# Graph layers on one core: the adjacency loaded as bf16 through GpSimd's queue into six half-size buffers

## The chip, the cores and the metric

The kernel runs on one core of one Trainium2 chip. The metric is the device time of one execution, in microseconds (us). TensorE (PE, with its weight loads shown apart as PEld), VectorE (DVE), ScalarE (ACT) and GpSimd (POOL) compute; SyncE (SP) and GpSimd start DMA transfers, which 16 DMA engines carry out. The engines run on their own instruction streams and meet at semaphores.

## The reference

There are 4096 nodes with 128 features, and an int32 adjacency of 4096 x 4096 in which an entry is 1 with probability 1/256. Two layers follow one another:

```python
def _L0_gnn_ref(x, adj):            # for each row: the maximum over its neighbours
    mask = a != 0
    masked = jnp.where(mask[:, :, None], x[None, :, :], neg)
    m = jnp.max(masked, axis=1)
...
def _L1_gnn_ref(input, W, a, adj, M):
    h = input @ W
    e = jax.nn.leaky_relu((h[:M] @ a_src)[:, None] + (h @ a_dst)[None, :], negative_slope=ALPHA)
    valid = (adj[:M] > 0) & (h.sum(axis=1) != 0)[None, :]
    att = jax.nn.softmax(jnp.where(valid, e, NEG), axis=1)
...
    attention = jnp.where(att >= THR, att, 0.0) * L[:, None]
    h_prime = attention @ h
    return jax.nn.elu(h[:M] + h_prime)
x = _layernorm(x + _L0_gnn_ref(x, adj), axis=-1)
x = _layernorm(x + _L1_gnn_ref(x, L1_gnn_W, L1_gnn_a, adj, 4096), axis=-1)
```

## The kernel before

**Tiling.** The 4096 rows of the adjacency are 32 tiles of 128; four tiles (512 rows) are a group, so there are 8 groups. The 4096 columns are 33 segments of 126, put together in 6 parts of 6, 6, 6, 5, 5 and 5 segments (PARTS). A part of a group is one load: 128 partitions x 4 tiles x up to 756 int32 (1512, 1260 or 1136 KB), in rows of up to 3024 bytes.

**First phase, to about 690 us.** For each segment of each group TensorE transposes the four 126-column blocks into psT (turn, L864 to L878), ScalarE turns them into 0/1 in bf16 (evict, L684, tile at), TensorE ranks them (rank, L884), ScalarE makes a one-hot choice (heat, L692, tile hot), and TensorE selects rows of x with it by three bf16 matmuls (select, L900, psS), whose running maximum DVE keeps (best, L1227, acc). This gives the maximum over one neighbour of each segment for each row. Small matmuls (code, L911) collect where further neighbours are. One group later DVE ranks these codes (top_keys, decode, make_lists at steps s = 1 to 7), and GpSimd gathers the rows of x by index from DRAM: 20 direct gathers (gather_direct, L621) and 12 extra ones (gather_extra, L631), each 128 rows of 512 bytes. DVE takes them in with direct_max (s = 30 of the same group) and extra_rows (L1374, s = 4 of the next one); TensorE's route (L945) and acc_turn, and DVE's aggregate (y, L1390, s = 9) follow, then the layer norm, x1 and the heads for the second layer. GpSimd may begin the gathers of a group only when the previous group's acc_turn has been taken, which y's instruction tells it.

**Order.** All orders are written by hand: each engine walks through g (groups, two more than 8) and s (33 segments), and what belongs to group g-1 or g-2 stands at fixed s. TensorE is two turns ahead of the selection.

**Queues.** The adjacency lands in adj_in, three buffers of one part each (ADJ_RING = 3). SP's queue carries all plain transfers. SP issues load q+3 when part q has been turned (semaphore turned), then the store of part q of at to adjT_dram (L474), and at the fourth part of a group the store of x1 (L483) and the load of own (L479). GpSimd's queue carries the gathers only. One semaphore, at_stored, counts all stores of at; evict waits on it before it writes a part of at again.

**Second phase.** From about 690 to 1010 us the attention reads at back from adjT_dram and reuses adj_in's bytes as wbuf (three float32 buffers; the total size of adj_in stays the same under the change). Then one block of rows is worked out exactly, and the kernel ends.

The code of the parts named is printed here.

## Time and profile before

| what | value |
|---|---|
| median of 3 runs | 1084.57 us (1081.44 to 1092.72) |
| the profiled execution | 1078.43 us, its span 1076.5 us |
| TensorE, DVE, ScalarE, GpSimd busy | 779.5, 675.2, 609.9, 272.1 us |
| TensorE's granted clock, mean | 0.885 of full speed |
| DMA, q1 (SP) and q0 (GpSimd) | 148.98 MB at 40.4%, 19.02 MB at 16.3% of 16 engines' time |
| HBM read, written | 129.11 MB, 40.96 MB |

A row of the time line gives start and duration in us, engine, line and operation, out<-in with shapes, and in brackets how long the engine was idle before it and who released it. A row of the windows gives, for a stretch A:B, its length, then busy us and count of instructions for PE, PEld, DVE, ACT and POOL, then the granted TensorE clock, the mean busy share of the 16 DMA engines, and GB/s. Times count from the start of the span.

### The profile page before, as it was taken

The numbers are of one execution on the slowest core, as the hardware profiler recorded it, in microseconds if no ns is written. First come the engines' busy times: TensorE is split into PE (matmuls) and PEld (weight loads), VectorE is DVE, ScalarE is ACT, GpSimd is POOL, SyncE is SP. The second block draws the span as 40 slices with busy tenths as digits, with TensorE's granted clock in tenths as the row PEclk, the third lists the DMA queues.
The fourth block names the chain that finished last, engine by engine and source line by source line (L and its number), as shares of the span: only waits on it lengthen the run. The fifth ranks groups of instructions, "written<-read, shape, count | busy, mean of one in ns | idle before, by whom it ended". The sixth has DMA issues, their size and how long they took to land.

```text
span 1076.5 us, 16405 instructions
## 1 busy us (share of the span) xinstructions
PE 779.5 (72%) x5872; PEld 595.6 (55%) x5935; DVE 675.2 (63%) x1662; ACT 609.9 (57%) x1257; POOL 272.1 (25%) x275
## 2 busy tenths in 40 slices
PE   1698976957968959659779320399989899998615
PEld 0365644634635636436446120298889888888314
DVE  6558577557666766656675812648667766865371
ACT  1886663834835726526537100557977977885413
POOL 7100732713705607407417274000000000000000
PEclk9999998989979989979989655599999999999757
DMA  9287796894985976956977525531442354151200
GB/s 331 88 268 238 218 187 209 232 210 137 268 208 157 235 209 194 187 188 203 195 235 189 49 67 30 182 122 35 173 168 73 123 181 143 40 181 36 90 0 5
DMA packets 69154, 169.08 MB, mean 157 GB/s; under 512 B 7311, under 2 KB 27920, under 8 KB 68912
## 3 DMA queue, kind: packets, MB, share of 16 engines
q1 hardware_dynamic: 60672, 148.98, 40.4%
q0 software_dynamic: 8400, 19.02, 16.3%
q8 instruction: 50, 0.82, 0.3%
q14 instruction: 32, 0.26, 0.1%
HBM read 129.11 MB, written 40.96 MB: 158 GB/s over the span
## 4 chain that ended last, share of the span: by engine, by line
PE 42%; DVE 27%; DMA 13%; issue 9%; ACT 6%; POOL 3%; DVEq 0%; POOLq 0%
DMA adj_in<-in_adj_dram 12%; PE psS L900 11%; PE psT L1049 7%; DVE adj_in L1490 7%; PE psT L875 7%; PE psR L1049 6%; ACT adj_in L768 3%; PE psR L884 2%; DVE acc L1227 2%; POOL G L621 1%; DVE ident L1171 1%; DVE wide L1327 1%; PE psR L1115 1%; DVE listed L1323 1%; PE psS L945 1%
## 5 line engine op out<-in xcount | busy, mean ns | idle before, releaser
L684 ACT ACTIVATE at<-psT 126x512 bf16<-126x512 int32 (+1 forms) x264 | 157.4, 597 | 222.3 <-PE psT L875 221.7
L1227 DVE TENSOR_TENSOR acc<-acc,psS 128x512 f32<-128x512 f32 x248 | 168.9, 684 | 170.9 <-PE psS L900 170.2
L900 PE MATMUL psS<-hot,x_split 128*128 128x512 bf16 x774 | 224.0, 395 | 39.9 <-DVE acc L1227 23.6
L875 PE MATMUL psT<-ident,adj_in 128*126 128x128 f32 (+1 forms) x1056 | 177.0, 293 | 44.2 <-DMA adj_in<-in_adj_dram 44.2
L621 POOL DMA_INDIRECT G<-x_tab_dram,idx x128 | 121.3, 948 | 334.5 <-DVE y L1390 231.6
L1490 DVE SCALAR_TENSOR_TENSOR adj_in<-adj_in,at 128x3072 f32<-128x3072 f32 (+1 forms) x48 | 148.3, 3090 | 70.6 <-ACT adj_in L768 70.6
L768 ACT ACTIVATE adj_in<-acc,minus,r_col 128x512 f32<-128x512 f32 x264 | 189.3, 803 | 2.5 <-PE psT L1049 2.5
L692 ACT ACTIVATE hot<-psR 128x512 bf16<-128x512 f32 x264 | 156.3, 592 | 0.2 <-PE psR L884 0.2
L875 PEld LDWEIGHTS psT<-ident,adj_in 128*126 128x126 f32 (+1 forms) x1056 | 121.5, 148 | 50.2 <-DMA adj_in<-in_adj_dram 44.7
L1049 PE MATMUL psT<-h_seg,adj_in 128*128 128x130 f32 x1056 | 126.3, 281 | 21.0 <-DVE adj_in L1490 20.6
L900 PEld LDWEIGHTS psS<-hot,x_split 128*128 128x128 bf16 x792 | 75.5, 100 | 118.8 <-DVE acc L1227 32.1
L1049 PEld LDWEIGHTS psT<-h_seg,adj_in 128*128 128x128 f32 x1056 | 122.7, 195 | 25.6 <-issue 14.0
L1049 PE MATMUL psR<-h_seg,adj_in 128*128 128x130 f32 x1056 | 125.6, 279 | 14.1 <-DVE adj_in L1490 13.8
L1049 PEld LDWEIGHTS psR<-h_seg,adj_in 128*128 128x128 f32 x1056 | 121.4, 193 | 17.1 <-DVE adj_in L1490 16.2
L911 PEld LDWEIGHTS psC<-codebook,at 128*128 128x128 bf16 x1056 | 67.0, 99 | 67.4 <-issue 8.8
L631 POOL DMA_INDIRECT G<-x_tab_dram,idx_extra x96 | 94.3, 982 | 29.3 <-issue 29.3
L884 PE MATMUL psR<-at,first 128*128 128x512 bf16 x219 | 87.8, 401 | 12.0 <-ACT at L684 12.0
L643 POOL DMA_INDIRECT adj_in<-in_adj_dram,exact_idx x1 | 0.9, 944 | 351.1 <-DVE exact_idx L1602 351.1
L945 PE MATMUL psS<-CT,extra_max 128*128 128x512 f32 x16 | 13.9, 966 | 76.9 <-issue 76.9
L911 PE MATMUL psC<-codebook,at 128*128 128x19 bf16 x1056 | 67.0, 173 | 0.0
L692 ACT ACTIVATION_READ_ACCUMULATOR hot<-psR 128x1 f32 x264 | 53.9, 204 | 0.0
L945 PEld LDWEIGHTS psS<-CT,extra_max 128*128 128x128 f32 x16 | 3.4, 264 | 77.6 <-issue 77.6
(272 smaller groups left out, 876.9 us busy)
## 6 DMA issues: line engine op xcount, KB each, us to landing
adj_in<-in_adj_dram SPq DMA_DIRECT2D x24, 1512.0 KB, 14.3
adj_in<-in_adj_dram SPq DMA_DIRECT2D x16, 1260.0 KB, 7.2
adjT_dram<-at SPq DMA_DIRECT2D x24, 768.0 KB
at<-adjT_dram SPq DMA_DIRECT2D x24, 768.0 KB, 7.9
adjT_dram<-at SPq DMA_DIRECT2D x24, 640.0 KB
at<-adjT_dram SPq DMA_DIRECT2D x24, 640.0 KB, 5.3
adj_in<-in_adj_dram SPq DMA_DIRECT2D x8, 1136.0 KB, 7.1
own<-in_x_dram SPq DMA_DIRECT2D x8, 256.0 KB
```

Source lines behind the costliest of these rows:

```text
L621: pool.indirect_dma_start(out=G[:, k * GT + t, :] if k < 4 else gmax[:, t, :], out_offset=None, in_=x_tab, in_offset=bass.IndirectOffsetOn ...
L631: pool.indirect_dma_start(out=G[:, 4 * GT + k, :], out_offset=None, in_=x_tab, in_offset=bass.IndirectOffsetOnAxis(ap=idx_extra[:, k:k + 1 ...
L684: nc.scalar.activation(at[0:w, s, :], psT[0:w, n % 2, :].bitcast(I32), ACT.Sign).then_inc(at_ready, 1)
L692: nc.scalar.activation(hot[:, n % 3, :], psR[:, n % 2, :], ACT.Relu, accum_out=hot_sums[:, n:n + 1]).then_inc(hot_ready, 1)
L768: nc.scalar.activation(wbuf[:, q % 3, s - s0, :], rho[:, g % 2, :], ACT.Relu, bias=minus1[:, :], scale=r_col[:, s:s + 1]).then_inc(relu_re ...
L875: mm = nc.tensor.transpose(psT[0:w, n % 2, t * P:(t + 1) * P], adj_in[:, q % ADJ_RING, t, (s - s0) * SEG:(s - s0) * SEG + w].bitcast(F32), ...
L884: nc.tensor.matmul(psR[:, n % 2, :], first[:, :], at[:, n % SEGS, :], start=True, stop=True).then_inc(ranked, 1)
L900: mm = nc.tensor.matmul(psS[:, b, :], x_split[:, k, s, :], hot[:, n % 3, :], start=(k == 0), stop=(k == 2))
L911: mm = nc.tensor.matmul(code_bank(q)[:, t * (s1 - s0) + s - s0, :], at[:, s, t * P:(t + 1) * P], codebook[:, s, :], start=True, stop=True)
L1049: mm = nc.tensor.matmul(psN[g % 2][:, t // 2, (t % 2) * HPAD:(t % 2) * HPAD + D + 2], wbuf[:, q % 3, s - s0, t * P:(t + 1) * P], h_seg[:, ...
L1227: V.tensor_tensor(acc[:, b, :], acc[:, b, :], psS[:, b, :], ALU.max).then_inc(free[b], 1)
L1490: V.scalar_tensor_tensor(out=wbuf[:, q % 3, 0:m, :], in0=wbuf[:, q % 3, 0:m, :], scalar=1.0, in1=at_ring[q % 5][:, 0:m, :], op0=ALU.add, o ...
```

## The change

The adjacency is loaded by GpSimd's queue instead of SP's, with conversion from int32 to bf16 by the DMA. adj_in holds bf16 in six buffers of one part, each half as many bytes as before, so a load waits for the part six earlier. TensorE's transposes take bf16 data and a bf16 identity (ident_bf, made by one more DVE instruction) and write bf16 into the first half of the psT bank; ScalarE's evict reads that. The loads stand at fixed places among GpSimd's gathers. The semaphore at_stored becomes one for each part.

```diff
-ADJ_RING = 3
+ADJ_RING = 6
...
-        adj_in = sb("adj_in", [P, ADJ_RING, GT, PART * P], I32)
+        adj_in = sb("adj_in", [P, ADJ_RING, GT, PART * P], BF16)
+        ident_bf = sb("ident_bf", [P, P], BF16)
...
-        at_stored = sem("at_stored")
+        at_stored = [sem(f"at_stored{k}") for k in range(NPARTS)]
...
         @block.gpsimd
         def _(pool):
+            def load_adj(q):
+
+                g, k = q // NPARTS, q % NPARTS
+                if q >= GROUPS * NPARTS:
+                    return
+                c0, c1 = PARTS[k][0] * SEG, min(PARTS[k][1] * SEG, N)
+                if q >= ADJ_RING:
+                    before_q = q - ADJ_RING
+                    pool.wait_ge(turned, before_q // NPARTS * SEGS + PARTS[before_q % NPARTS][1])
+                pool.dma_start(adj_in[:, q % ADJ_RING, :, 0:c1 - c0], adj_g[g][:, :, c0:c1]
+                               ).then_inc(adj_loaded[q % ADJ_RING], 16)
+
+            load_adj(0)
             pool.memset(xs, ABSENT).then_inc(x_blank, 1)
+            load_adj(1)
...
+            load_adj(2)
             pool.wait_ge(consts_pool, 8)
             pool.memset(at[96:P, 0:SEGS - 1, :], 1.0).then_inc(consts_pool, 1)
 
+            for q in range(3, ADJ_RING):
+                load_adj(q)
...
                 for t in range(GT):
+                    if t == 2:
+                        load_adj((g + 2) * NPARTS + 2)
...
+                load_adj((g + 2) * NPARTS + 3)
                 for k in range(EXTRA):
+                    if k == EXTRA // 2:
+                        load_adj((g + 2) * NPARTS + 4)
...
+            for k in range(NPARTS):
+                load_adj(NPARTS + k)
             for g in range(GROUPS):
+                load_adj((g + 2) * NPARTS)
+                load_adj((g + 2) * NPARTS + 1)
                 gather_direct(g)
                 gather_extra(g)
+                load_adj((g + 2) * NPARTS + 5)
...
-                    act.wait_ge(at_stored, 16 * (q + 1))
+                    act.wait_ge(at_stored[PART_OF[s]], 16 * g)
                 w = width(s)
-                nc.scalar.activation(at[0:w, s, :], psT[0:w, n % 2, :].bitcast(I32), ACT.Sign).then_inc(at_ready, 1)
+                nc.scalar.activation(at[0:w, s, :], psT[0:w, n % 2, :].bitcast(BF16)[:, 0:ROWS], ACT.Sign).then_inc(at_ready, 1)
...
                 for t in range(GT):
-                    mm = nc.tensor.transpose(psT[0:w, n % 2, t * P:(t + 1) * P],
-                                             adj_in[:, q % ADJ_RING, t, (s - s0) * SEG:(s - s0) * SEG + w].bitcast(F32),
-                                             ident[:, :])
+                    mm = nc.tensor.transpose(psT[0:w, n % 2, :].bitcast(BF16)[:, t * P:(t + 1) * P],
+                                             adj_in[:, q % ADJ_RING, t, (s - s0) * SEG:(s - s0) * SEG + w],
+                                             ident_bf[:, :])
...
+            V.tensor_copy(ident_bf[:, :], ident[:, :])
```

On GpSimd, the instructions of the second group's gathers, before (G and gmax are the tiles that gathers fill, idx and idx_extra the index lists):

```order
L621 DMA G<-x_tab_dram,idx 128x128 [waits free1,list_ready]
L621 DMA G<-x_tab_dram,idx 128x128 x3
L621 DMA gmax<-x_tab_dram,idx 128x128
L621 DMA G<-x_tab_dram,idx 128x128 x4
L621 DMA gmax<-x_tab_dram,idx 128x128
...
L631 DMA G<-x_tab_dram,idx_extra 128x128 [waits extra_ready,free1]
L631 DMA G<-x_tab_dram,idx_extra 128x128 x11
```

The same place in the changed kernel (line numbers are the changed kernel's; L583 is the load):

```order
L583 DMA adj_in<-in_adj_dram 128x4x756 [waits turned] x2
L628 DMA G<-x_tab_dram,idx 128x128 [waits free1,list_ready]
...
L583 DMA adj_in<-in_adj_dram 128x4x756 [waits turned]
...
L583 DMA adj_in<-in_adj_dram 128x4x630 [waits turned,extra_ready,free1]
L641 DMA G<-x_tab_dram,idx_extra 128x128 x6
L583 DMA adj_in<-in_adj_dram 128x4x630 [waits turned]
L641 DMA G<-x_tab_dram,idx_extra 128x128 x6
L583 DMA adj_in<-in_adj_dram 128x4x568 [waits turned]
```

Two loads now stand ahead of the first gather, one behind the tenth, one ahead of the extra gathers, one in their middle and one behind them, and each waits for the part six earlier to be turned.

On SP, the start of the program before (h_seg is where x lands first):

```order
L468 DMA adj_in<-in_adj_dram 128x4x756
L487 DMA h_seg<-in_x_dram 126x32x128 [waits x_blank]
L489 DMA h_seg<-in_x_dram 64x128
L468 DMA adj_in<-in_adj_dram 128x4x756
L491 DMA w_aug<-in_L_gnn_W_dram 128x128
L493 DMA a<-in_L_gnn_a_dram 128x1
L494 DMA a<-in_L_gnn_a_dram 128x1
L468 DMA adj_in<-in_adj_dram 128x4x756
L496 DMA x_tab_dram<-in_x_dram 32x16384
```

and in the changed kernel:

```order
L478 DMA h_seg<-in_x_dram 126x32x128 [waits x_blank]
L480 DMA h_seg<-in_x_dram 64x128
L481 DMA w_aug<-in_L_gnn_W_dram 128x128
L483 DMA a<-in_L_gnn_a_dram 128x1
L484 DMA a<-in_L_gnn_a_dram 128x1
L485 DMA x_tab_dram<-in_x_dram 32x16384
```

The loads of the adjacency are gone from this queue; what is left keeps its order.

## Rows read from the trace of the kernel before

**Rows 1.** Windows by group: length, PE, PEld, DVE, ACT, POOL, PEclk, DMA share, GB/s.

```profile
332.00:405.00 73.00, 57.78 (x426) 37.80 (x433) 49.75 (x151) 40.29 (x105) 30.28 (x32) 0.92 0.80 206
405.00:486.00 81.00, 57.74 (x427) 37.86 (x434) 49.63 (x151) 40.82 (x105) 30.59 (x32) 0.88 0.75 190
```

**Rows 2.** The page, part 4: the chain that ended last, shares by line.

```profile
DMA adj_in<-in_adj_dram 12%; PE psS L900 11%; PE psT L1049 7%; DVE adj_in L1490 7%; PE psT L875 7%; PE psR L1049 6%; ACT adj_in L768 3%; PE psR L884 2%; DVE acc L1227 2%; POOL G L621 1%; DVE ident L1171 1%; DVE wide L1327 1%; PE psR L1115 1%; DVE listed L1323 1%; PE psS L945 1%
```

**Rows 3.** Time line of GpSimd: first gathers of four groups, last gathers of two.

```profile
107.33 1.11 POOL L621 DMA_INDIRECT G<-x_tab_dram,idx  x1 [66.30 <-DVE idx L1331]
332.13 0.94 POOL L621 DMA_INDIRECT G<-x_tab_dram,idx  x1 [33.44 <-DVE y L1390]
370.92 0.94 POOL L631 DMA_INDIRECT G<-x_tab_dram,idx_extra  x1 [0.30 <-issue]
405.36 0.94 POOL L621 DMA_INDIRECT G<-x_tab_dram,idx  x1 [33.50 <-DVE y L1390]
560.54 0.94 POOL L621 DMA_INDIRECT G<-x_tab_dram,idx  x1 [34.30 <-DVE y L1390]
659.37 0.94 POOL L631 DMA_INDIRECT G<-x_tab_dram,idx_extra  x1 [0.30 <-issue]
```

**Rows 4.** Time line of DVE: extra_rows (L1374) three times, y (L1390) once.

```profile
387.62 0.96 DVE L1374 TENSOR_TENSOR G<-G 128x768 f32<-128x768 f32 x1 [2.11 <-DMA G<-x_tab_dram,idx_extra]
403.93 0.68 DVE L1390 TENSOR_TENSOR y<-psS,gmax 128x512 f32<-128x512 f32 x1
468.62 0.94 DVE L1374 TENSOR_TENSOR G<-G 128x768 f32<-128x768 f32 x1
667.41 0.96 DVE L1374 TENSOR_TENSOR G<-G 128x768 f32<-128x768 f32 x1 [17.90 <-DMA G<-x_tab_dram,idx_extra]
```

**Rows 5.** Waits to 600 us (total, times, longest); TensorE's time line at two stalls.

```profile
PE psT L875 <- DMA adj_in<-in_adj_dram: 44.2, 5, 14.5
...
380.51 1.11 PE L875 MATMUL psT<-ident,adj_in 128*126 128x128 f32 x4 [4.83 <-DMA adj_in<-in_adj_dram]
463.70 1.11 PE L875 MATMUL psT<-ident,adj_in 128*126 128x128 f32 x4 [14.49 <-DMA adj_in<-in_adj_dram]
```

**Rows 6.** DMA queues in 284 to 358, then 344 to 388: packets, MB, share.

```profile
q1 hardware_dynamic: 5137, 13.39, 52.2%
q0 software_dynamic: 1044, 2.14, 26.2%
...
q1 hardware_dynamic: 3468, 8.13, 53.6%
q0 software_dynamic: 768, 1.57, 43.2%
```

**Rows 7.** The line of the extra gathers: min/median/max ns.

```profile
L631 POOL DMA_INDIRECT G<-x_tab_dram,idx_extra x96: 940/944/1996, 132.9 to 659.4; - x96
```

**Rows 8.** Time line of TensorE: one free-running segment, and the next one's start.

```profile
197.90 0.64 PE L875 MATMUL psT<-ident,adj_in 128*126 128x128 f32 x4
198.37 0.38 PE L884 MATMUL psR<-at,first 128*128 128x512 bf16 x1
198.59 0.81 PE L900 MATMUL psS<-hot,x_split 128*128 128x512 bf16 x3
199.34 0.64 PE L875 MATMUL psT<-ident,adj_in 128*126 128x128 f32 x4
```

**Rows 9.** Time line of ScalarE: first and last of the three instructions of one segment.

```profile
44.53 0.60 ACT L684 ACTIVATE at<-psT 126x512 bf16<-126x512 int32 x1 [0.26 <-PE psT L875]
...
45.51 0.20 ACT L692 ACTIVATION_READ_ACCUMULATOR hot<-psR 128x1 f32 x1
```

**Rows 10.** The start: GpSimd's memset, DVE's ident, TensorE's first wait.

```profile
6.42 13.75 POOL L604 MEMSET at<- 32x16384 bf16 x1
6.39 13.85 DVE L1171 TENSOR_SCALAR ident<-before 128x128 f32<-128x128 f32 x1 [5.11 <-POOL row_id L601]
...
PE psS L972 <- DVE codebook L1202: 23.1, 1, 23.1
```

More of the change, by code:

```diff
@@ L461, in _ @@
         def _(sp):
-            def load_adj(q):
-                g, k = q // NPARTS, q % NPARTS
-                c0, c1 = PARTS[k][0] * SEG, min(PARTS[k][1] * SEG, N)
-                if q >= ADJ_RING:
-                    before_q = q - ADJ_RING
-                    sp.wait_ge(turned, before_q // NPARTS * SEGS + PARTS[before_q % NPARTS][1])
-                sp.dma_start(adj_in[:, q % ADJ_RING, :, 0:c1 - c0], adj_g[g][:, :, c0:c1]
-                             ).then_inc(adj_loaded[q % ADJ_RING], 16)
             def store_part(q):
@@ L473, in store_part @@
                 sp.wait_ge(at_ready, g * SEGS + PARTS[k][1])
-                sp.dma_start(adjT[g][:, PARTS[k][0]:PARTS[k][1], :], at_part(k)).then_inc(at_stored, 16)
+                sp.dma_start(adjT[g][:, PARTS[k][0]:PARTS[k][1], :], at_part(k)).then_inc(at_stored[k], 16)
             def load_own(g):
@@ L483, in store_x1 @@
                 sp.dma_start(x1_g[g], x1w[:, :, :]).then_inc(x1_stored, 16)
-            load_adj(0)
             sp.wait_ge(x_blank, 1)
@@ L489, in _ @@
             sp.dma_start(xs[0:LAST, SEGS - 1, :], x[(SEGS - 1) * SEG:N, :]).then_inc(x_loaded, 16)
-            load_adj(1)
             sp.dma_start(w_aug[:, 0:D], W).then_inc(weights_loaded, 16)
@@ L494, in _ @@
                 sp.dma_start(a3[:, 2:3], a[0:D, :]).then_inc(weights_loaded, 16)
-            load_adj(2)
             sp.dma_start(x_tab[1:N + 1, :], x).then_inc(tab_stored, 16)
@@ L504, in _ @@
                     if q < GROUPS * NPARTS:
-                        if q + ADJ_RING < GROUPS * NPARTS:
-                            load_adj(q + ADJ_RING)
                         store_part(q)
@@ L511, in _ @@
                             load_own(g - 1)
-            sp.wait_ge(at_stored, 16 * GROUPS * NPARTS)
+            for k in range(NPARTS):
+                sp.wait_ge(at_stored[k], 16 * GROUPS)
             sp.wait_ge(x1_stored, 16 * GROUPS)
@@ L634, in gather_extra @@
                     ).then_inc(extra_gathered, 16)
+            for k in range(NPARTS):
+                load_adj(NPARTS + k)
             for g in range(GROUPS):
+                load_adj((g + 2) * NPARTS)
+                load_adj((g + 2) * NPARTS + 1)
                 gather_direct(g)
                 gather_extra(g)
+                load_adj((g + 2) * NPARTS + 5)
             pool.wait_ge(ex_listed, 1)
```

## The prediction

> **What bounds the kernel now.** I read the windows by group first. Between 107 and 560 us the kernel goes through six like groups of four row tiles, and in none of them is an engine full: in the two shown DVE works 50 of 73 and of 81 us, TensorE 58 of each, and the 16 DMA engines are busy 0.75 to 0.80 of the time [rows 1]. So a cycle of waits sets the pace. The shares of the chain name the DMA load of the adjacency first, with 12.1% [rows 2]. That is one chain; where two waits end together it shows only one of them, so I followed the other.
>
> GpSimd starts the gathers of a group when DVE has taken the turned maxima (y, L1390), and the starts stand at 107.33, 332.13, 405.36 and 560.54 us [rows 3]: six cycles in 453.2 us, 75.5 us each. Inside one of them: 32 gathers are issued from 332.13 to 371.9 (39.7 us, one per 1.25 us); DVE's extra_rows (L1374) waits for the last of them until 387.62, 15.7 us after its issue; y is written at 403.93, and the next gathers start at 405.36, 17.7 us after extra_rows [rows 3, 4]. 39.7 + 15.7 + 17.7 = 73.1: this closes the cycle without one adjacency load in it. The adjacency matters in a second way. TensorE stands idle for it five times, 44.2 us in all, the longest 14.5 [rows 5]. In the cycle from 332.13 its stall ends at 380.5, before the gathers' landing at 387.6, so it costs little. In the cycle from 405.36 it ends at 463.7 and extra_rows, at 468.62, waits for nothing any more: 63.3 us after the start instead of 55.4, so 8 us of the 14.5 count [rows 3 to 5].
>
> Why the last gather takes 15.7 us to land: with no other large traffic it takes 7.1 (660.3 to 667.41) [rows 3, 4]. From 344 to 388 us the engines spend 0.536 of their time on SP's queue and 0.432 on GpSimd's, 97% together [rows 6]: the gathers land when a backlog of loads and stores allows it.
>
> **The change, part by part.** *The ring.* Six buffers of half the bytes in place of three. A load is still issued when a part has been turned, but it is now needed a whole group later, not half a group. The stalls of [rows 5] go if the DMA engines keep up; the cover is a full cycle of about 70 us. What is late next is the gathers' landing, which is already the cycle.
>
> *The landing.* Loads and gathers now share one queue and are served in order, with stores beside them. Behind the last gather come the loads of part 5 and of the next part 0 (1136 and 1512 KB); ahead of it those of parts 2, 3 and 4 (1512, 1260, 1260 KB, 4.13 MB). SP's queue moves 13.39 MB in 0.522 of 74 us, so 347 GB/s while it works; gathers take 0.262, 19.4 us [rows 6]. In the stretch 344 to 388 SP's queue moved 8.13 MB; after the change what must be done before the last gather is 4.13 MB of loads, about 2.8 MB of stores (four parts) and 0.5 MB of x: 7.4 MB, so 0.7 MB or 2 us less. The landing comes 53.4 us after the start instead of 55.4, if a converted load costs the engines what a plain one does. I write r for that ratio: 4.13 MB at 347 GB/s are 11.9 us, so the landing is at 53.4 + 11.9 (r - 1). The trace has no converting load. From below r is 0.5 (half the bytes are written). From above the nearest row is GpSimd's own queue: 2.14 MB in 19.4 us, 110 GB/s, so r = 3.2; but its pieces are 512 bytes and a load's 3024, so I work the slow case at 2 and keep the far end for the range. I choose 1, since the bytes read from HBM are the same.
>
> *GpSimd.* Each load is issued by software there. The nearest row is a gather: 0.94 us for 128 pieces, 1.25 with its gap [rows 3, 7]. A load has 512 pieces, so a price c lies between 1.25 and four times 0.94 + 0.3 = 4.1; I take 2.0, nearer to the low end, as a gather must also read its indices. Three loads (parts 2, 3, 4) stand between the gathers, so the last one leaves at 39.7 + 3c = 45.7, and with 7.1 us of its own landing it is there at 52.8 at the earliest: just hidden under 53.4. The other three cost 6 us of GpSimd's idle 33 us. The waits on turned that are now ahead of gathers do not bind: part 2 is freed about 10 us after the start, and its load is behind ten gathers (12.5 us).
>
> *TensorE.* In a free-running segment four float32 transposes start at 197.90, the ranking at 198.37, the selection at 198.59 and the next segment at 199.34 [rows 8]: 0.47 us of 1.44 for the transposes. The ranking's 512 bf16 columns take 0.22, so 4 x 128 bf16 columns should take 0.22, 0.25 less, and the segment 1.19. ScalarE's three instructions leave room for just that: the first starts at 44.53, the last at 45.51 and ends at 45.7 [rows 9]. In the first group, where nothing else binds, 33 x 0.25 = 8 us. Inside a cycle it is worth little, since there the landing is waited for. I let it shorten the 17.7 us from extra_rows to the next start by 1.2 (five segments), to 16.5. If a transpose gains nothing, that is 8 + 7 us less.
>
> *The start.* TensorE's first work waits 23.1 us for DVE's codebook, and DVE's ident, ready at 6.4, takes 13.85 us beside GpSimd's memset of at [rows 10]. Three loads now stand before the end of that memset: 3c = 6 us later. Loads 1 and 2 now also run beside x and the weights instead of behind them. The bound from below is 0, as load 2 leaves DVE a gap before the memset.
>
> *The sum.* A cycle is 53.4 + 16.5 = 69.9 instead of 75.5; six of them give 34 us. The first group gives 8, the start takes 6. The two last groups have no loads beside them, and the attention phase is not touched: 0. 34 + 8 - 6 = 36 less. The profiled execution has 1078.4 us, so 1042; the median of the runs is 6.1 above it, so 1048.
>
> **A rule that speaks against it.** In [rows 7] 96 gathers take 944 ns in the median, 940 at least, 1996 at most, while DVE is busy two thirds of the time [rows 1]: hardly one was held up. The reverse does show: DVE's ident lasts 13.85 us beside a GpSimd memset [rows 10]. The Trainium skill (SBUF — State Buffer, Who interferes with whom) says that VectorE in a two-port mode keeps GpSimd from writing DMA descriptors for the whole instruction, and advises the hardware queues instead. By that rule, the trace agrees at most in the one slow gather, and the rival below has its price.
>
> **Rivals.**
> Slower: *the conversion is slow in the DMA engines* (r = 2). The landing comes at 65.3 us and the cycle is 81.8; the engines' own total is 19.4 + 48.4 for loads + 14.4 for the rest = 82.2, so 82.2 binds: 40 us more over six cycles. The first group then needs about 60 us of DMA where TensorE needs 39 (10 to 15 us net of its gain), and the start loses 13 + 6. Together about 60 more: 1145. It decides from r = 1.47 on, where the cycle is 75.5 again. For it: nothing in the trace shows the rate. Against it: equal bytes read. 0.24.
> No change: *the stalls go, the gathers do not land earlier.* Either c is 4 (the last gather leaves at 52, lands at 59) or the gathers wait behind all loads in their own queue. The cycle is 75 to 76: 1075 to 1090. Against it: that the landing follows from the engines' total, which the order does not change. 0.14.
> *DVE locks GpSimd out while it writes descriptors.* If each of the three loads waits 1.05 us more (1996 - 944), the last gather leaves at 48.9 and lands at 56.0: cycle 72.5, 1064. The page named above is the reason to list it. 0.05.
> Faster: *a converted load costs its written bytes* (r = 0.5) and c is 1.25. Then GpSimd binds: 39.7 + 3.8 + 7.1 = 50.6, cycle 67.1, 50 us over six, start 4: about 54 less, 1031. 0.13.
>
> **How the numbers follow.** The forecast itself has 0.44, with 1034 to 1064 as its own range (c and the start at either end, the transposes with or without their gain). About 1% is what a measurement can tell from no change. Below 1074 lie the forecast, the lock-out and the faster case: 0.62. Within 1% the no-change case: 0.14. Above, the slow conversion: 0.24. The range of 8 in 10 must reach into both sides: from 1024 to 1130, which leaves out the slow case beyond about r = 1.8 and up to the 3.2 of the far bound.
>
> **What would show it.** Right: no DMA wait at the transposes' line; a load's issue on GpSimd near 2 us; extra_rows 53 us after a group's first gather, with a wait of 5 us or more ahead of it; starts 70 us apart; segments of 1.2 us in the first group; the DMA share near 0.8 with the same read bytes. Wrong: a DMA share near 1 in every group with fewer GB/s (slow conversion), issues of 4 us, or gathers that land 20 us after their issue.

## The result, and the profile after

The changed kernel takes 1094.5 us in the median (1090.8 to 1100.2), the kernel before, in the same comparison, 1084.0: 1.011 times as long, with a 95% interval from 1.008 to 1.013. The forecast was 1048. So the change costs about 1% where 3.3% less was expected; the time lies inside the range, on its other side.

The page of the changed kernel, parts 1 and 3 (busy us of each engine; then queue, packets, MB and the share of the 16 engines' time):

```profile
span 1089.3 us, 16472 instructions
PE 747.4 (69%) x5935; PEld 544.9 (50%) x5935; DVE 675.8 (62%) x1663; ACT 607.9 (56%) x1257; POOL 314.7 (29%) x323
...
DMA packets 69154, 135.53 MB, mean 124 GB/s; under 512 B 7311, under 2 KB 52496, under 8 KB 68912
...
q0 software_dynamic: 33744, 52.58, 34.0%
q1 hardware_dynamic: 35328, 81.86, 22.0%
...
HBM read 129.11 MB, written 40.96 MB: 156 GB/s over the span
```

What the change does to each part is there: TensorE has 32 us less to do, GpSimd 43 us more, and the loads have moved from q1 to q0 with 33.6 MB less moved (169.08 before). None of that sets the time. One cycle does, the one that starts at 414.20. First GpSimd's time line (L628 and L641 are the gathers, L583 the loads), then DVE's (L1377 direct_max, L1390 extra_rows, L1406 y):

```profile
414.20 1.02 POOL L628 DMA_INDIRECT G<-x_tab_dram,idx  x1 [5.80 <-DVE y L1406]
...
426.52 0.83 POOL L583 DMA_DIRECT2D adj_in<-in_adj_dram  x1
...
439.89 0.84 POOL L583 DMA_DIRECT2D adj_in<-in_adj_dram  x1
...
448.26 0.83 POOL L583 DMA_DIRECT2D adj_in<-in_adj_dram  x1
449.39 1.69 POOL L641 DMA_INDIRECT G<-x_tab_dram,idx_extra  x1 [0.30 <-issue]
...
456.57 0.94 POOL L641 DMA_INDIRECT G<-x_tab_dram,idx_extra  x1 [0.30 <-issue]
...
493.37 1.01 POOL L628 DMA_INDIRECT G<-x_tab_dram,idx  x1 [5.80 <-DVE y L1406]
```

```profile
449.02 1.22 DVE L1377 TENSOR_TENSOR G<-G 128x1024 f32<-128x1024 f32 x1
474.69 0.96 DVE L1390 TENSOR_TENSOR G<-G 128x768 f32<-128x768 f32 x1 [11.12 <-DMA G<-x_tab_dram,idx_extra]
491.93 0.68 DVE L1406 TENSOR_TENSOR y<-psS,gmax 128x512 f32<-128x512 f32 x1
```

The last gather is issued 42.4 us after the first and is taken in at 60.5 us (this moment is called the landing from here on), behind a wait of 11.12 us. Before, such a wait was 2.11 us [rows 4]. The waits for the same thing over the whole span, of the kernel before and then of the changed one (total, times, longest; the last group's 17.9 is in both):

```profile
DVE G L1374 <- DMA G<-x_tab_dram,idx_extra: 28.3, 6, 17.9
DVE G L1390 <- DMA G<-x_tab_dram,idx_extra: 82.1, 8, 17.9
```

In the six cycles extra_rows comes 60.1, 60.5, 58.3, 56.4, 60.5 and 59.6 us after the first gather, 59.2 in the mean. Before it was 55.1 to 56.6 in four cycles and 61.3 and 63.3 in the two that an adjacency load held up, 57.8 in the mean. The starts of the gathers stand at 105.67 and, six cycles later, at 571.61: 77.7 us each, against 75.5 [rows 3]. That is 12.7 us in six cycles. The start is 1.7 us earlier (105.67 against 107.33), what follows the six cycles is 1.7 longer: together 12.8, the difference of the spans (1089.3 and 1076.5).

What the engines do in the wait. The windows (length, PE, PEld, DVE, ACT, POOL busy, granted clock, DMA share, GB/s) of the changed kernel, a whole cycle and then from the last gather's issue to its landing, with the queues of the same stretch:

```profile
414.20:493.40 79.20, 55.00 (x435) 32.10 (x434) 49.85 (x151) 40.20 (x104) 36.29 (x39) 0.82 0.77 142
457.50:474.70 17.20, 2.31 (x19) 1.17 (x19) 5.88 (x16) 2.17 (x6) 1.66 (x3) 0.72 1.00 138
```

```profile
q0 software_dynamic: 1119, 1.52, 88.2%
q1 hardware_dynamic: 158, 0.85, 11.9%
```

and the queues of the kernel before from its last gather's issue to its landing, 371.9 to 387.6:

```profile
q0 software_dynamic: 221, 0.42, 60.3%
q1 hardware_dynamic: 545, 1.83, 34.9%
```

TensorE works 2.3 of 17.2 us there, and its mean granted clock is 0.72 of 2.4 GHz. All 16 DMA engines are taken, 88% of their time by GpSimd's own queue, and they move 138 GB/s, where SP's queue reached 347 while it worked [rows 6]. That low rate is not new, as the window of the kernel before from its last gather's issue to its landing shows (a converted load counts here with the bf16 bytes that it writes):

```profile
371.90:387.60 15.70, 9.22 (x54) 5.59 (x54) 9.63 (x25) 5.86 (x15) 0.00 (x0) 0.78 0.96 145
```

Every DMA packet stands in the trace with its start, its queue, its duration and its size, and the size tells a gather's packets (4096 bytes) from those of a load (1512, 1260 or 1136). Of the 17.2 us, the gathers' packets take 8.0 us of all 16 engines, the load of part 4, which stands ahead of the last six gathers, 1.8, the loads behind the last gather 5.3, and SP's queue 2.1. (The 5.3 fall, by the order of the queue, on engines that are through with their share of the gathers.) The order in the queue shows most clearly at the load of part 2: from 429 to 433 us GpSimd's queue serves 303 packets of it and not one of a gather, though three gathers had been issued behind it by 431.2. So the gathers wait in their own queue behind loads, and what they themselves do is slow.

### The profile page after: what moved, and what is told of

It is laid out like the page before. It is cut to its first block, busy times and chain, and to the rows that moved or that the text cites. A ratio compares the mean times of both kernels' runs of the same rounds, so it can differ in the third digit from the quotient of the medians.

```text
span 1089.3 us, 16472 instructions
## 1 busy us (share of the span) xinstructions
PE 747.4 (69%) x5935; PEld 544.9 (50%) x5935; DVE 675.8 (62%) x1663; ACT 607.9 (56%) x1257; POOL 314.7 (29%) x323
## 3 DMA queue, kind: packets, MB, share of 16 engines
q0 software_dynamic: 33744, 52.58, 34.0%
q1 hardware_dynamic: 35328, 81.86, 22.0%
## 4 chain that ended last, share of the span: by engine, by line
PE 19%; DVE 17%; issue 7%; ACT 4%; POOL 3%; DMA 1%; DVEq 0%; POOLq 0%
PE psT L1064 7%; DVE adj_in L1506 7%; PE psR L1064 6%; ACT adj_in L783 3%; POOL G L628 1%; PE psR L1130 1%; POOL G L641 1%; DVE G L1526 1%; DMA G<-x_tab_dram,idx_extra 1%; DVE stats L1559 1%; PE psS L1111 1%; PE psC L1045 1%; PE psS L1035 1%; DVE G L1556 1%; DVE G L1553 1%
## 5 line engine op out<-in xcount | busy, mean ns | idle before, releaser
L699 ACT ACTIVATE at<-psT 126x512 bf16<-126x512 bf16 (+1 forms) x264 | 157.6, 597 | 229.3 <-PE psT L890 218.9
L915 PE MATMUL psS<-hot,x_split 128*128 128x512 bf16 x792 | 230.4, 402 | 53.2 <-DVE acc L1243 36.8
L628 POOL DMA_INDIRECT G<-x_tab_dram,idx x128 | 123.0, 961 | 117.1 <-DVE y L1406 77.3
L915 PEld LDWEIGHTS psS<-hot,x_split 128*128 128x128 bf16 x792 | 66.7, 101 | 146.6 <-DVE acc L1243 49.0
L1064 PE MATMUL psR<-h_seg,adj_in 128*128 128x130 f32 x1056 | 125.6, 279 | 14.2 <-DVE adj_in L1506 13.8
L1064 PEld LDWEIGHTS psR<-h_seg,adj_in 128*128 128x128 f32 x1056 | 121.4, 193 | 17.2 <-DVE adj_in L1506 16.3
L890 PE MATMUL psT<-ident_bf,adj_in 128*126 128x128 bf16 (+1 forms) x1056 | 117.0, 237 | 0.0
L899 PE MATMUL psR<-at,first 128*128 128x512 bf16 x264 | 107.2, 406 | 13.2 <-ACT at L699 13.2
L960 PE MATMUL psS<-CT,extra_max 128*128 128x512 f32 x16 | 16.4, 1125 | 144.0 <-issue 144.0
L641 POOL DMA_INDIRECT G<-x_tab_dram,idx_extra x96 | 96.9, 1010 | 29.2 <-issue 29.2
L926 PEld LDWEIGHTS psC<-codebook,at 128*128 128x128 bf16 x1056 | 67.4, 99 | 69.9 <-issue 13.0
L890 PEld LDWEIGHTS psT<-ident_bf,adj_in 128*126 128x126 bf16 (+1 forms) x1056 | 89.2, 145 | 7.2 <-issue 7.0
L583 POOL DMA_DIRECT2D adj_in<-in_adj_dram x48 | 38.4, 806 | 186.3 <-PE psT L890 185.5
```

The source lines that it names most:

```text
L628: pool.indirect_dma_start(out=G[:, k * GT + t, :] if k < 4 else gmax[:, t, :], out_offset=None, in_=x_tab, in_offset=bass.IndirectOffsetOn ...
L641: pool.indirect_dma_start(out=G[:, 4 * GT + k, :], out_offset=None, in_=x_tab, in_offset=bass.IndirectOffsetOnAxis(ap=idx_extra[:, k:k + 1 ...
L699: nc.scalar.activation(at[0:w, s, :], psT[0:w, n % 2, :].bitcast(BF16)[:, 0:ROWS], ACT.Sign).then_inc(at_ready, 1)
L890: mm = nc.tensor.transpose(psT[0:w, n % 2, :].bitcast(BF16)[:, t * P:(t + 1) * P], adj_in[:, q % ADJ_RING, t, (s - s0) * SEG:(s - s0) * SE ...
L899: nc.tensor.matmul(psR[:, n % 2, :], first[:, :], at[:, n % SEGS, :], start=True, stop=True).then_inc(ranked, 1)
L915: mm = nc.tensor.matmul(psS[:, b, :], x_split[:, k, s, :], hot[:, n % 3, :], start=(k == 0), stop=(k == 2))
```

## The experiments

Cycle is the mean of the six from the first group's first gather; landing the mean, in those cycles, from a group's first gather to extra_rows. The ratio is to the kernel before on the same chip; its median there was 1095 us for a_int, after_2 and a_behind_2 (on a second chip), 1082 for the other four ending in _2 and 1087 for the rest (one chip, at two times). Where spread is in the name, extra_rows waits for no gather, and the column shows only when DVE came to it; in a_all_2 the first gather has another place, so it has no landing to compare.

| kernel | median us | ratio, 95% | landing | cycle |
|---|---|---|---|---|
| a_behind | 1033.9 | 0.946 to 0.958 | 50.2 | 68.3 |
| a_behind_2 | 1044.1 | 0.947 to 0.967 | 51.3 | 69.4 |
| a_34_2 | 1042.1 | 0.954 to 0.968 | 50.6 | 68.9 |
| a_lite_2 | 1057.0 | 0.967 to 0.981 | 53.5 | 71.9 |
| a_int | 1096.5 | 1.001 to 1.008 | 59.7 | 77.9 |
| after_2 | 1098.9 | 1.003 to 1.010 | 60.6 | 78.9 |
| b_bfturn | 1082.8 | 0.990 to 0.998 | 59.1 | 77.1 |
| b_spread | 1033.8 | 0.944 to 0.958 | 52.6 | 71.1 |
| a_spread | 1024.0 | 0.935 to 0.947 | 49.3 | 67.9 |
| a_behind_spread_2 | 1028.4 | 0.941 to 0.955 | 49.1 | 67.9 |
| a_all_2 | 1024.6 | 0.938 to 0.952 | | 66.9 |

The theory after the two traces were compared: the loads that stand ahead of the last gather in its own queue delay it (order). The rivals: the converting loads hold the DMA engines longer (conversion), the three issues take GpSimd's time (issue), or the engines are full whatever the order (total, which is what the forecast had assumed).

**a_behind: the order alone.** In the changed kernel the loads of parts 2, 3 and 4 go behind the last extra gather. Nothing else changes, so bytes, conversion and total stay.

```diff
-                    if t == 2:
-                        load_adj((g + 2) * NPARTS + 2)
...
-                load_adj((g + 2) * NPARTS + 3)
                 for k in range(EXTRA):
-                    if k == EXTRA // 2:
-                        load_adj((g + 2) * NPARTS + 4)
...
                 gather_extra(g)
-                load_adj((g + 2) * NPARTS + 5)
+                for k in range(2, NPARTS):
+                    load_adj((g + 2) * NPARTS + k)
```

> The changed kernel with the loads of parts 2, 3 and 4 moved behind the last extra gather (parts 0 and 1 stay ahead of the first). Theory 'order in the shared queue': in the changed kernel the last gather lands 59.2 us after the first one is issued, 5.8 later than forecast, because 128-piece gathers stand behind 8 us of loads in their own ring; with the loads behind them the landing comes at 50 to 54 us, the cycle falls from 77.7 to 69-72 us and the kernel runs about 1045 to 1060. Rival 'engines' total': the same bytes are moved per cycle, so the landing stays within 2 us of 59 or the wait moves to the adjacency (a DMA wait at the transposes), and the time stays at 1085 to 1095.

It is 4.8% faster than the kernel before, 1034 us and a cycle of 68.3, a little better than the 1045 to 1060 and 69 to 72 that were expected. Its time line, one cycle (GpSimd's first and last gather, DVE's extra_rows):

```profile
378.33 1.02 POOL L626 DMA_INDIRECT G<-x_tab_dram,idx  x1 [5.17 <-DVE y L1402]
...
417.88 0.94 POOL L636 DMA_INDIRECT G<-x_tab_dram,idx_extra  x1 [0.30 <-issue]
...
428.41 0.96 DVE L1386 TENSOR_TENSOR G<-G 128x768 f32<-128x768 f32 x1 [1.01 <-DMA G<-x_tab_dram,idx_extra]
```

The landing falls from 59.2 to 50.2 us, and no wait of the transposes for the adjacency appears: six buffers leave the time for a load that is issued up to 28 us later (part 2: 40.5 us after the first gather instead of 12.3). The same engines carry the same bytes (52.58 and 81.86 MB), so the rival total is refuted, and with it that the engines had no room: what was wrong was the order. On another chip (a_behind_2) the ratio repeats, with a landing of 51.3 and 1044 us, just above the ranges expected:

> A repeat of a_behind beside a_int and the changed kernel on one chip. If the order in the queue is the cause, it repeats: extra_rows 49 to 51 us after the first gather, cycles of 68 to 69, 1028 to 1042. Were the gain of the first run one of its chip, it would fall within 2% of the changed kernel: 1070 to 1095.

**a_34_2: which of the loads.** Parts 3 and 4 go behind, part 2 stays behind the tenth gather.

```diff
-                load_adj((g + 2) * NPARTS + 3)
                 for k in range(EXTRA):
-                    if k == EXTRA // 2:
-                        load_adj((g + 2) * NPARTS + 4)
...
-                load_adj((g + 2) * NPARTS + 5)
+                for k in range(3, NPARTS):
+                    load_adj((g + 2) * NPARTS + k)
```

> A repeat of a_34 on another chip: the changed kernel with the loads of parts 3 and 4 behind the last extra gather, that of part 2 still ahead of it (1.5 MB, behind the tenth of 32 gathers). Theory of the bytes ahead: part 2 is served while the other direct gathers are still being issued, so it costs little; the landing is close to that with all three behind (a_behind: 48.6 to 51.2 us), 50 to 52; 1035 to 1048. Rival 'each load costs the same, in issue or in bytes': a third of the way from 49.9 to 59.2, so 53; cycles of 71.4, 1052.

Landing 50.6: the load of part 2 costs 0.4 us, less than two runs of one kernel differ by (50.2 and 51.3, 59.2 and 60.6), and the two that stand at the extra gathers cost the other 8.6 of 9.0. An equal price per load (53, 1052) is refuted. In the changed kernel's trace the packets of part 2 are served from 429 to 435 us, 14 us before the first extra gather is issued.

**a_lite_2: bytes against issue.** The changed kernel, but from the third group on the loads of parts 2, 3 and 4 bring only 126 columns per row. The rest is left from earlier groups, so the result is not the adjacency's.

```diff
                 c0, c1 = PARTS[k][0] * SEG, min(PARTS[k][1] * SEG, N)
+                if g >= 2 and k in (2, 3, 4):
+                    c1 = c0 + SEG
```

> A repeat of a_lite on another chip (the first one ran where the kernel before needed 1281 us, with waits that chip 15 did not show). The changed kernel, but from the third group on the loads of parts 2, 3 and 4 bring 126 columns of each row only; the rest of those parts is what an earlier group left, so part of the adjacency is wrong in value. Number, order and descriptors of the loads stay as in the changed kernel: 0.77 MB stand ahead of the last gather in the queue instead of 4.13. Theory 'the bytes ahead of the gathers in their own queue': extra_rows 50 to 52 us after a group's first gather instead of 59, cycles of 68 to 70, about 1035 (1025 to 1050). Rival 'the issue of the loads on GpSimd' (3 x 1.13 us and what DVE adds): landing stays at 58 to 59 us, 1085 to 1095. Rival 'the engines as a whole are full': the landing moves in proportion to all traffic, 3.4 of about 13 MB less a cycle, so about 54 us, 1060.

Its time line in one cycle, the same three instructions:

```profile
394.35 1.02 POOL L630 DMA_INDIRECT G<-x_tab_dram,idx  x1 [3.40 <-DVE y L1408]
...
436.54 0.94 POOL L643 DMA_INDIRECT G<-x_tab_dram,idx_extra  x1 [0.30 <-issue]
...
449.10 0.96 DVE L1392 TENSOR_TENSOR G<-G 128x768 f32<-128x768 f32 x1 [7.47 <-DMA G<-x_tab_dram,idx_extra]
```

The landing is 53.5 and the time 1057 us: the 1035 of the theory was missed by 22, and both numbers are those of the third rival, the engines as a whole (54 and 1060). This run alone cannot tell the two apart, since fewer bytes are both less in the queue and less in all; a_behind can, where the bytes in all are the same and the landing falls by 9.0 us. What it does show is that the bytes are not the whole of the 9.0. The last gather is issued 42.2 us after the first here, as in the changed kernel, but 39.6 in a_behind. So 5.7 of the 9.0 us go with the bytes of the three loads. Of the other 3.3, about 2.6 would be their issue on GpSimd if the landing follows the last issue one for one, which no run tests alone, and 0.7 is left (the small loads still have 512 pieces each). Each is good to about 1 us, as two runs of one kernel show. The bytes are the larger part; the rival issue may be true for a good quarter.

**a_int: queue without conversion.** The changed kernel with an int32 adj_in of three buffers, TensorE still turning in bf16 (a view of the low halves). Its loads stand at the same places under the same waits, for the part three lower.

```diff
-ADJ_RING = 6
+ADJ_RING = 3
...
-        adj_in = sb("adj_in", [P, ADJ_RING, GT, PART * P], BF16)
+        adj_in = sb("adj_in", [P, ADJ_RING, GT, PART * P], I32)
...
-                        load_adj((g + 2) * NPARTS + 2)
+                        load_adj((g + 2) * NPARTS + 2 - 3)
```

> The changed kernel's queue and order without its conversion: the adjacency stays int32 in three buffers, its loads are issued on GpSimd at the same places, each under the same wait (the index of the part is three lower), and TensorE still turns in bf16 (a strided view of the low halves). Theory 'the order in one ring': the same bytes read are ahead of the last gather, so extra_rows comes 58 to 61 us after a group's first gather, as in the changed kernel (59.2), cycles of 76 to 79. With three buffers the parts come just in time, so adjacency stalls return and may add: 1090 to 1115. Rival 'the conversion makes the loads hold the engines or the ring longer': extra_rows 53 to 56 us after the first gather (55.4 in the kernel before), 1050 to 1082.

Beside the changed kernel on one chip:

> The changed kernel itself, beside the others on one chip: cycles of 77 to 78 us, extra_rows 59 us after the first gather, 1085 to 1100; a ratio of 1.005 to 1.015 to the kernel before on this chip.

The time line of a_int in one cycle, then TensorE's wait for the adjacency over its span (total, times, longest), then the queue of GpSimd on its page:

```profile
421.04 1.00 POOL L629 DMA_INDIRECT G<-x_tab_dram,idx  x1 [3.78 <-DVE y L1407]
...
463.38 0.94 POOL L642 DMA_INDIRECT G<-x_tab_dram,idx_extra  x1 [0.30 <-issue]
...
478.85 0.96 DVE L1391 TENSOR_TENSOR G<-G 128x768 f32<-128x768 f32 x1 [2.46 <-DMA G<-x_tab_dram,idx_extra]
```

```profile
PE psT L891 <- DMA adj_in<-in_adj_dram: 53.1, 12, 9.6
```

```profile
q0 software_dynamic: 21456, 86.13, 32.0%
```

1096.5 us against 1098.9, landing 59.7 against 60.6: without any conversion the loss is the same, so the conversion does not make it. It is the same even though TensorE now waits 53.1 us for the adjacency; extra_rows still waits 2.5 to 4.9 us for the gathers in each of the six cycles, so those waits are covered by the landing. The conversion itself costs little. By the sizes of their packets the 48 loads took 212 us of all 16 engines in the kernel before (SP's queue), 203 in the changed kernel (converted, GpSimd's queue; 191 in a_behind) and 177 in a_int (the same queue, not converted, in half as many packets of twice the piece).

**b_spread and a_spread: why a gather is so slow.** Where a list is shorter than its places, the place holds index 0, the row of absent values, one row of 512 bytes in DRAM. Here these places point at 128 equal rows behind the table, a different one for each partition. It costs four small DVE instructions a group in place of two, one more at the start, and a store of 64 KB.

```diff
+            V.tensor_scalar(pad_row[:, :], part_id[:, :], float(N + 1), None, ALU.add)
...
-                V.tensor_copy(idx_extra[:, :], psS[:, b, 0:EXTRA]).then_inc(free[b], 1)
+                a = mark(V.scalar_tensor_tensor(out=pad_extra[:, :], in0=psS[:, b, 0:EXTRA], scalar=0.0,
+                                                in1=pad_row[:, :].to_broadcast([P, EXTRA]),
+                                                op0=ALU.is_equal, op1=ALU.mult))
+                after(a)
+                V.tensor_tensor(idx_extra[:, :], pad_extra[:, :], psS[:, b, 0:EXTRA], ALU.add).then_inc(free[b], 1)
```

(the same for idx, and 128 rows more in x_tab). In the kernel before:

> The kernel before, but an empty place in a gather list points to one of 128 equal rows (a row of its own for each partition) instead of all to row 0 of the table; two small DVE instructions and one store of 64 KB more. Theory 'one hot row': 4 KB packets of the last extra gathers take 1.2 to 1.7 us each although others take 0.16 to 0.3, with or without other traffic, since nearly all their indices are the same DRAM row; with the rows spread the last gather lands 3 to 7 us after its issue instead of 15.7, extra_rows no longer waits, the six adjacency stalls then set the cycle: 66 to 71 us instead of 75.5, about 1045 to 1060. Rival 'traffic': the packets are slow from loads and stores beside them; the landing stays near 15 us and the time at 1084.

and in the changed kernel:

> The changed kernel with the same spreading of the empty places. Theory 'one hot row': the landing falls from 16 to 4-8 us after the last issue, and as the deeper ring leaves no adjacency stall, the cycle becomes 43 + 6 + 18 = 65 to 68 us instead of 77.7; about 1020 to 1035, and faster than the kernel before with spread rows. Rival 'order in the shared queue': gathers still stand behind 8 us of loads, the landing comes down by 3 us at most, 1070 or more. Rival 'traffic': no change, 1094.

The last gathers of the program, with no other traffic beside them. The kernel before, 644 to 667.4 us:

```profile
DMA packets 447, 0.91 MB, mean 39 GB/s; under 512 B 224, under 2 KB 224, under 8 KB 447
q0 software_dynamic: 447, 0.91, 61.5%
```

b_spread, 619 to 636 us, and then its queue over the whole span, from its page:

```profile
q0 software_dynamic: 430, 0.85, 17.9%
```

```profile
q0 software_dynamic: 8400, 19.02, 5.9%
```

447 packets take 0.615 x 23.4 x 16 = 230 us of engine time, 0.52 each; with spread rows 430 take 49 us, 0.11 each. Over the span q0's share falls from 16.3% to 5.9% with the same 19.02 MB. So most of the gathers' DMA time was the one repeated row, and the rival traffic is refuted. (The profiled execution of b_spread took 1046 us, more than its median of 1034, so its cycle of 71.1 is rather high.) One thing came otherwise than expected: the adjacency stalls do not set the cycle of b_spread, they are gone. Its trace has no wait of the transposes for a load, where the kernel before has 44.2 us of them with the same loads, ring and queue [rows 5]. So the slow gathers made those stalls too, and 1034 us is better than the 1045 to 1060 expected. Without the repeated row the kernel before is 4.9% faster and the changed one 5.9%, with its loads still ahead of the gathers. In the changed kernel with spread rows (time line of DVE, then windows):

```profile
426.12 0.94 DVE L1403 TENSOR_TENSOR G<-G 128x768 f32<-128x768 f32 x1
```

```profile
387.00:397.00 10.00, 9.42 (x86) 5.75 (x86) 6.24 (x15) 8.55 (x23) 7.84 (x9) 1.00 0.79 176
397.00:407.00 10.00, 9.74 (x94) 6.19 (x95) 5.70 (x11) 8.94 (x24) 7.87 (x9) 1.00 0.86 219
407.00:417.00 10.00, 9.03 (x88) 5.28 (x89) 8.69 (x16) 8.19 (x22) 7.87 (x9) 1.00 1.00 250
417.00:427.00 10.00, 5.38 (x52) 2.88 (x49) 9.69 (x26) 5.07 (x14) 4.17 (x5) 1.00 0.92 207
```

extra_rows waits for nothing. TensorE is nearly full until 417 and DVE is after it: work, not a landing, now sets the 68 us.

**a_behind_spread_2 and a_all_2: do the two add?** The first has both edits (their diffs are above).

> A repeat on another chip: the changed kernel with both edits, the loads of parts 2, 3 and 4 behind the last extra gather and the empty places of the lists pointing at 128 rows of the table instead of one. Each alone gave 1034 and 1024 on chip 15. If both act on one wait (the gathers' landing), they do not add: cycles of 67 to 68 set by DVE's work, 1020 to 1030. If they were two separate costs, the gains would add (52 and 64 us): 975 to 985.

1028.4 us, cycle 67.9: no better than a_spread, so both act on the one wait, as expected. The second also issues the 16 gathers into G without waiting for the maxima of the group before:

```diff
-                if g:
-                    wait_taken(pool, "acc_turn", g - 1)
...
-                    for k in range(DIRECT):
+                    for k in range(DIRECT - 1):
...
+                if g:
+                    wait_taken(pool, "acc_turn", g - 1)
+                for t in range(GT):
+                    pool.indirect_dma_start(
+                        out=gmax[:, t, :], out_offset=None, in_=x_tab,
```

> A repeat on another chip: both edits, and the 16 gathers of a group that write G issued as soon as the list is ready, without the wait for the maxima of the group before; the four of the fifth place wait for it, behind them. If DVE's own work of a cycle (about 50 us busy, in order) and what it waits for on TensorE bind now, not the issue of 32 gathers on GpSimd (40 us), the cycle falls little: 64 to 67 us, 1000 to 1025. If the issue on GpSimd was still part of the closed cycle, up to 20 gathers' issue (25 us) leaves it and DVE's busy time is next: 55 to 60 us, 955 to 985.

1024.6: next to nothing more. The cycle is 66.9 us, 1.0 shorter, but the first group's first gather comes 3.9 us later (109.96 against 106.11). The time line shows how little the edit freed: the gathers now wait for their list (L1357), which DVE has ready at 374.3, 3 us before y at 377.5.

```profile
374.57 1.02 POOL L628 DMA_INDIRECT G<-x_tab_dram,idx  x1 [1.63 <-DVE idx L1357]
```

**b_bfturn: the transposes alone.** The kernel before, with bf16 transposes from a strided view of its int32 buffers.

```diff
-                                             adj_in[:, q % ADJ_RING, t, (s - s0) * SEG:(s - s0) * SEG + w].bitcast(F32),
-                                             ident[:, :])
+                                             adj_bf[:, q % ADJ_RING, t, (s - s0) * SEG:(s - s0) * SEG + w, 0],
+                                             ident_bf[:, :])
```

> The kernel before with only TensorE's transposes changed: they read the low half of each int32 of adj_in as bf16 (a stride of two elements), with a bf16 identity, and write bf16; loads, ring and queues as before. Theory: a free-running segment falls from 1.44 to about 1.2 us, which is worth 6 to 8 us in the first group and nothing inside the cycles of 75 us, since the gathers' landing and the adjacency stalls take it up: 1076 to 1080. Rival 'transposes matter everywhere': 33 segments x 8 groups x 0.25 = 60 us, about 1025. Rival 'the strided read costs it': no change or slower.

TensorE's wait for the adjacency over its span:

```profile
PE psT L877 <- DMA adj_in<-in_adj_dram: 69.9, 6, 16.2
```

0.6% faster (0.990 to 0.998). The first gather of the first group comes 4.7 us earlier, at 102.61; this is less than the 6 to 8 expected. After that the cycles are no shorter (77.1 in the profiled run, 75.5 before): TensorE waits for the loads 69.9 us in six waits where there were 44.2 in five [rows 5].

**Four runs on a disturbed chip.** a_34, a_lite, a_behind_spread and a_all first ran where the kernel before took 1281 us, 18% more than elsewhere, with waits of up to 27 us in their traces that no other trace has (those of DVE's acc, ScalarE's at and others for what the profile calls remote). Their ratios, 0.982, 0.938, 0.985 and 0.959, order the kernels in another way than the repeats do, and no conclusion rests on them, nor on what was expected of them.

## Why the prediction was wrong, point by point

- **The cycle of waits** that it found (gathers, landing, y) is the one that sets the time. Right: all the kernels that shorten the landing are faster by it, and it explains the 12.8 us.
- **The ring.** Right: the wait of the transposes for the adjacency is gone from the changed kernel (44.2 us before). It was rightly called late next to the landing.
- **The landing is the step that failed.** The text took the old landing, 55.4, and subtracted 2 us for 0.7 MB less ahead of it; 53.4 was forecast, it is 59.2. In its terms the last gather was to leave later and the time from its issue to the landing to shrink from 15.7 us to 7.7. Only the first happened: the last gather starts 42.5 us after the first in the mean of the six cycles (39.2 before), and from there it is 16.7 us to extra_rows, where the four cycles before that no adjacency load held up had 16.3. What kept it long is the order in the queue, for which the subtraction of bytes had no term. The forecast kept the overlap of the kernel before, where at the landing the engines had gathers in one queue (60.3%) and SP's transfers in another (34.9%). Afterwards loads and gathers are one line, and with the same bytes in the other order (a_behind) the landing is 9.0 us earlier and only 10.4 us behind the start of the last issue. The Trainium skill (DMA: Bandwidth & Descriptors) says under Queues, rings and completion order that an engine takes turns between the queues it has work for, and under Two DMAs through the same engine are not ordered that within one queue of one engine descriptors start in order. The trace agrees: no gather packet among 303 of the load ahead of it. The last group's gathers from 644 us on, with the twelve extra ones, need 0.615 x 23.4 = 14.4 us of all engines, most of it for the one row; a load ahead of such gathers comes on top.
- **The rival that came true** is the gathers that wait behind all loads in their own queue. Its mechanism was named and had a chance of 0.14, priced as no gain: a cycle of 75 to 76, 1075 to 1090. The cycle is 77.7 and the time 1094.5, so even this price was too low. The sentence that spoke against it, that the landing follows from the engines' total, which the order does not change, is what a_behind refutes.
- **r = 1** was right: the loads took 212 us of the engines before, 203 after. The slow conversion, which had 0.24, is refuted by that and by a_int. (Its sum was also off: 40, 10 to 15, 13 and 6 are 69 to 74, not about 60. Nothing else used it.)
- **GpSimd.** A load's issue is 0.83 us with no gap ahead of it, 1.13 with the gap of the next instruction; 2.0 was forecast, and even the low end of 1.25 was too high. With 39.7 + 3 x 1.13 = 43.1 the last gather should leave at 43; it does at 43.3 (457.51) instead of 45.7. Being held up by DVE, another rival, is small: the 96 extra gathers take 1010 ns in the mean, against 982 on the page of the kernel before (median 944 [rows 7]), though in each group one of them now takes 1.2 to 1.9 us. In the cycle shown the landing came 17.2 us behind the last issue, where the forecast allowed 7.7.
- **TensorE.** Right in size. A free-running segment takes 1.23 us (forecast 1.19, before 1.44 [rows 8]):

```profile
196.14 0.42 PE L890 MATMUL psT<-ident_bf,adj_in 128*126 128x128 bf16 x4
196.40 0.38 PE L899 MATMUL psR<-at,first 128*128 128x512 bf16 x1
196.62 0.81 PE L915 MATMUL psS<-hot,x_split 128*128 128x512 bf16 x3
...
197.37 0.42 PE L890 MATMUL psT<-ident_bf,adj_in 128*126 128x128 bf16 x4
```

  From extra_rows to the next start the changed kernel needs 17.9 to 18.7 us, 17.7 before. The 1.2 us expected there did not come. The wait is not the reason, since a_spread, which has none, needs 18.7 in the mean. DVE works 14.2 of the 18.7 us there (474.7 to 493.4) and 14.2 of 17.8 in the kernel before, so faster transposes could shorten little there; the rest of the stretch was not taken apart.
- **The start.** 8 - 6 = 2 us earlier was forecast, 1.7 came, and this is luck: both terms were some 2 us too large. TensorE's first wait is 27.4 us instead of 23.1 [rows 10], so the start costs 4.3: the three issues ahead of the memset put the codebook 3.0 us later, to 26.1, and then TensorE waits for the weights a, which land at 27.3 instead of 20.4. The first group then gained 6.0, not 8.

```profile
PE psS L987 <- DMA a<-in_L_gnn_a_dram: 27.4, 1, 27.4
```

- **The sum.** The span is 12.8 us longer instead of 36 shorter, 49 apart. Six cycles of 77.7 instead of 69.9 us are 47 of them.

What stays open: how the 9.0 us divide between bytes and issue to better than 1 us, what the last 0.7 of them are, and why a 4096-byte packet of a gather from one row takes as long as it does.

## What to carry to other kernels

Before a transfer is moved onto another queue, ask what in that queue is waited for, and put the move behind it; three loads with a whole cycle to spare cost 9 us a cycle for standing ahead of gathers that had none; with the three behind the gathers the kernel was 5% faster than before the change. A queue's share of the engines' time is no measure of what can lie beside it once it is one line: read the rate while the critical transfer is in flight. And where a gather pads its list, look at which address the padding hits.

## What the runs showed of the hardware

- A gather whose empty places all point at one row of DRAM holds the engines much longer than one with these places spread over 128 rows: in the last gathers of the program 0.52 against 0.11 us of engine time per packet, about 4.5 times (half of these packets carry 4 bytes). The 4096-byte packets of the extra gathers in the six cycles took 1.15 us in the mean of the kernel before and 0.17 in b_spread.
- In one queue a gather's packets wait for those of a load issued before it: 303 load packets and no gather packet in 4 us, with three gathers issued behind the load.
- Conversion from int32 to bf16 in a load is nearly free: the 48 loads took 203 us of the engines (191 in a_behind), 212 as plain loads on SP's queue and 177 unconverted on GpSimd's. Its issue takes as long with conversion as without (806 and 798 ns in the mean).
- A load of 512 pieces is issued by GpSimd in 0.83 us, less than a gather of 128 (0.94).
- 16 engines that are all busy moved 138 GB/s beside the gathers of one row (145 in the kernel before): a full DMA share says nothing of a rate.
